# Expert tiles of a ternary mixture-of-experts layer: regrouped scale factors and a square on GpSimd

## What is computed

```python
def activation_quant(x):
    scale = 127.0 / jnp.maximum(jnp.max(jnp.abs(x), axis=-1, keepdims=True), EPS)
    return jnp.clip(jnp.round(x * scale), -128.0, 127.0) / scale

def expert_ffn(x, gw, uw, dw):
    gate = bitlinear(x, gw)
    up = bitlinear(x, uw)
    activated = up * jnp.square(jax.nn.relu(gate))
    return bitlinear(activated, dw)

logits = x @ router_w.T
probs = jax.nn.softmax(logits, axis=-1)
top_w, top_i = jax.lax.top_k(probs, TOP_K)
top_w = top_w / jnp.sum(top_w, axis=-1, keepdims=True)
combine = jnp.sum(top_w[..., None] * jax.nn.one_hot(top_i, E, dtype=x.dtype), axis=1)
for e in range(E):
    y_e = expert_ffn(x, gate_w[e], up_w[e], down_w[e])
    out = out + combine[:, e:e + 1] * y_e
```

## Time and profile before

| what | value |
|---|---|
| median of three runs | 2146.79 us (2142.44 to 2147.7) |
| the profiled execution | 2147.27 us |
| its span on the core | 2145.4 us |
| busy share PE, DVE, ACT, POOL | 81%, 75%, 55%, 28% |
| phase of the experts, scatter of the rows | 1969.5 to 2008.9 us of the span |
| loop over expert tiles, first Relu to last output | 2017.3 to 2119.4 us |

### The profile page before, as it was taken

One profiled execution on the slowest core, in us unless ns is written; L12 is line 12 of the kernel. 1 busy time (PEld: TensorE's weight loads), 2 busy tenths in 40 slices (PEclk: granted clock), 3 DMA queues, 4 the chain that ended last, 5 costly groups with the idle time before them and its releaser, 6 DMA issues.

```text
span 2145.4 us, 46365 instructions
## 1 busy us (share of the span) xinstructions
PE 1733.8 (81%) x14186; PEld 1285.6 (60%) x14186; DVE 1608.5 (75%) x4372; ACT 1181.8 (55%) x3306; POOL 601.1 (28%) x734
## 2 busy tenths in 40 slices
PE   6999999999999977756657998989889787863373
PEld 6867777777777655633335666666667566643142
DVE  4578888888888845779965888888888368874396
ACT  1156556556556524444543766666667557652393
POOL 0022222222222200001102434343443135534342
PEclk9999999999999979977777999999999879985697
DMA  2011111111111150030002222222211100000124
GB/s 104 1 34 28 29 33 28 28 33 28 28 33 28 42 121 4 1 105 1 0 8 67 56 59 59 59 59 59 64 30 36 34 11 12 12 13 14 47 78 150
DMA packets 119516, 87.66 MB, mean 41 GB/s; under 512 B 76991, under 2 KB 95746, under 8 KB 118532
## 3 DMA queue, kind: packets, MB, share of 16 engines
q1 hardware_dynamic: 116484, 80.26, 14.2%
q0 software_dynamic: 2944, 6.37, 0.9%
HBM read 72.60 MB, written 12.21 MB: 40 GB/s over the span
## 4 chain that ended last, share of the span: by engine, by line
PE 45%; DVE 25%; issue 12%; ACT 12%; POOL 2%; DMA 1%; DVEq 1%; ACTq 1%; SPq 1%; POOLq 0%
PE ps L641 4%; PE ps L663 3%; PE ps L650 3%; PE ps L679 3%; PE ps L709 3%; PE ps L612 3%; PE ps L1900 3%; PE ps L1828 2%; ACT a_pr L393 2%; PE ps L978 2%; DVE d_ks L1697 2%; PE ps L1879 2%; PE ps L1838 2%; ACT d_pr L1631 1%; POOL f_row_store L2491 1%
## 5 line engine op out<-in xcount | busy, mean ns | idle before, releaser
L393 ACT ACTIVATE a_pr<-ps,a_nm 128x257 f32<-128x257 f32 x512 | 238.2, 473 | 173.4 <-DVE a_nm L508 173.4
L516 DVE COPY a_pT<-ps 128x512 f32<-128x512 f32 x256 | 170.2, 685 | 60.0 <-PE ps L679 59.5
L1651 ACT ACTIVATE d_pr<-d_st,d_nm 128x257 f32<-128x257 f32 x256 | 128.1, 502 | 128.7 <-DVE d_nm L1760 127.4
L508 DVE TENSOR_REDUCE a_nm<-ps 128x2 f32<-128x514 f32 x256 | 174.5, 682 | 0.0
L329 POOL TENSOR_TENSOR a_sf<-a_sf,a_ratio 128x256 f32<-128x256 f32 x64 | 39.4, 616 | 472.8 <-DVE a_ratio L537 472.8
L679 PE MATMUL ps<-ident,a_pr 128*128 128x128 f32 x1024 | 159.0, 278 | 0.0
L1879 PE MATMUL ps<-d_kc,d_qc 128*128 128x257 f32 x512 | 141.8, 400 | 14.6 <-DVE d_vc L1736 14.5
L641 PE MATMUL ps<-a_cT,a_wqk 128*128 128x257 f32 x512 | 133.7, 383 | 2.9 <-DVE a_k L481 1.7
L679 PEld LDWEIGHTS ps<-ident,a_pr 128*128 128x128 f32 x1024 | 120.6, 144 | 25.7 <-issue 12.7
L1559 POOL TENSOR_TENSOR d_kc<-d_kc,d_ks 128x257 f32<-128x257 f32 x64 | 60.2, 941 | 267.8 <-ACT d_dist L1616 133.3
L650 PE MATMUL ps<-a_wvg,a_cT 128*128 128x256 f32 x512 | 129.0, 395 | 0.0
(11 more groups left out here) (385 smaller groups left out, 4491.6 us busy)
## 6 DMA issues: line engine op xcount, KB each, us to landing
a_cT<-in_ctx SPq DMA_DIRECT2D x64, 257.0 KB, 2.6
d_cT<-in_ctx SPq DMA_DIRECT2D x64, 257.0 KB, 2.8
f_wf<-in_f_w SPq DMA_DIRECT2D x24, 512.0 KB, 3.8
a_vbd<-a_vself SPq DMA_DIRECT2D x256, 8.0 KB, 1.8
d_lp<-d_pr SPq DMA_DIRECT2D x256, 0.5 KB
e_vb<-e_vs SPq DMA_DIRECT2D x256, 8.5 KB, 1.8
f_yab<-f_y_store SPq DMA_DIRECT2D x16, 256.0 KB, 5.8
c_wf<-in_c_w SPq DMA_DIRECT2D x3, 1024.0 KB, 6.9
```

Source lines behind the costliest of these rows:

```text
L393: ins = act.activation(pr[j][:, g, :], ps[:, S_BANK[u % 2] + k, S:LK], ACT.Exp, bias=nm[j][:, g:g + 1], accum_out=ssum[j][:, 0, g:g + 1])
L508: dve.tensor_reduce(nm[j][:, 2 * u:2 * u + 2], ps[:, s0:s0 + 2, S:LK], AX.X, ALU.max, negate=True).then_inc(max_ready.sem, 1)
L516: dve.tensor_copy(pT[u][:, :, :, :], ps[:, T_BANK[u % 2], :].rearrange("p (g c q) -> p g c q", g=2, c=2))\
L1651: ins = act.activation(pr[j][:, g, :], st[u][:, k, :], ACT.Exp, bias=nm[u][:, k:k + 1], accum_out=sm[j][:, g:g + 1])
```

## The change

The factors that a stored row carries are regrouped. The word at `ROW - 4` held f (the product of the squared gate scale, the up scale and the cube of the row's input scale) and now holds EPS / (127 f); the word at `ROW - 3` is multiplied by 127 f. With them the scales of a set come from three small instructions where there were five: the larger of max / 127 and the new factor, its reciprocal, and the output's scale. The routing part has four chained instructions more, and a blank row's factor is 1. The square of the odd tile moves from ACT to POOL, as a multiplication of the Relu by itself, and is put in POOL's program one set ahead of the outputs: in turn u POOL squares the odd tile of set u and then scatters the outputs of set u - 2.

```diff
-        route_link, size_link2 = chain("f_route_link", 26), chain("f_size_link2", 3)
+        route_link, size_link2 = chain("f_route_link", 30), chain("f_size_link2", 1)
...
-        rg_done, sq_done, a_done = signal("f_rg_done", 2), signal("f_sq_done", 2), signal("f_a_done", 2)
+        rg_done, a_done = signal("f_rg_done", 2), signal("f_a_done", 2)
+        sq_done = [signal(f"f_sq_done{k}") for k in range(2)]
...
-            for u in range(SETS):
-                eng.wait_ge(y_even.sem, y_even.at(u, 1))
-                eng.wait_ge(y_odd.sem, y_odd.at(u, 1))
+            for u in range(SETS + 2):
+                if u < SETS:
+                    eng.wait_ge(rg_done.sem, rg_done.at(u, 2))
+                    if u >= 1:
+                        eng.wait_ge(a_done.sem, a_done.at(u - 1, 2))
+                    eng.tensor_tensor(rg2[1][:, :], rg[1][:, :], rg[1][:, :], ALU.mult).then_inc(sq_done[1].sem, 1)
+                if u < 2:
+                    continue
+                eng.wait_ge(y_even.sem, y_even.at(u - 2, 1))
+                eng.wait_ge(y_odd.sem, y_odd.at(u - 2, 1))
                 for k in range(2):
                     eng.indirect_dma_start(y_store[:, :],
-                                           bass.IndirectOffsetOnAxis(tile_in[u % HELD][:, k, ROW - 1:ROW], 0),
+                                           bass.IndirectOffsetOnAxis(tile_in[(u - 2) % HELD][:, k, ROW - 1:ROW], 0),
...
                 act.activation(rg[k][:, :], ps[:, 2 + 2 * k, :], ACT.Relu).then_inc(rg_done.sem, 1)
-                act.wait_ge(rg_done.sem, rg_done.at(u, k + 1))
+                if k == 1:
+                    return
+                act.wait_ge(rg_done.sem, rg_done.at(u, 1))
                 if u >= 1:
-                    act.wait_ge(a_done.sem, a_done.at(u - 1, k + 1))
-                act.activation(rg2[k][:, :], rg[k][:, :], ACT.Square).then_inc(sq_done.sem, 1)
+                    act.wait_ge(a_done.sem, a_done.at(u - 1, 1))
+                act.activation(rg2[0][:, :], rg[0][:, :], ACT.Square).then_inc(sq_done[0].sem, 1)
...
-            dve.tensor_tensor(rows_f[:, :, :, ROW - 4], got[:, 2, :, :], spread(xs3[:, :], 1, 2), ALU.mult)\
+            rl.link(dve, dve.tensor_tensor(got[:, 2, :, :], got[:, 2, :, :], spread(xs3[:, :], 1, 2), ALU.mult))
+            rl.link(dve, dve.tensor_scalar(got[:, 2, :, :], got[:, 2, :, :], 127.0, None, ALU.mult))
+            rl.link(dve, dve.reciprocal(picked[:, :, :, 0], got[:, 2, :, :]))
+            dve.tensor_scalar(rows_f[:, :, :, ROW - 4], picked[:, :, :, 0], EPS, None, ALU.mult)\
                 .then_inc(scales_ready.sem, 1)
...
-            dve.tensor_tensor(rows_f[:, :, :, ROW - 3], got[:, 1, :, :], got[:, 3, :, :], ALU.mult)\
+            rl.link(dve, dve.tensor_tensor(got[:, 1, :, :], got[:, 1, :, :], got[:, 3, :, :], ALU.mult))
+            dve.tensor_tensor(rows_f[:, :, :, ROW - 3], got[:, 1, :, :], got[:, 2, :, :], ALU.mult)\
                 .then_inc(scales_ready.sem, 1)
...
-                sl.link(dve, dve.tensor_tensor(a[:, 1, :], a[:, 0, :], factors[:, :, ROW - 4], ALU.mult))
-                sl.link(dve, dve.tensor_scalar(a[:, 1, :], a[:, 1, :], EPS, None, ALU.max))
-                sl.link(dve, dve.reciprocal(a[:, 2, :], a[:, 1, :]))
+                sl.link(dve, dve.scalar_tensor_tensor(a[:, 1, :], a[:, 0, :], 1.0 / 127.0, factors[:, :, ROW - 4],
+                                                      ALU.mult, ALU.max))
                 sl.end()
-                dve.scalar_tensor_tensor(a[:, 3, :], a[:, 2, :], 127.0, factors[:, :, ROW - 4], ALU.mult, ALU.mult)\
-                    .then_inc(size_done.sem, 1)
+                dve.reciprocal(a[:, 3, :], a[:, 1, :]).then_inc(size_done.sem, 1)
                 dve.tensor_tensor(a[:, 4, :], a[:, 1, :], factors[:, :, ROW - 3], ALU.mult)
...
+    o["f_blank"][:, ROW - 4] = np.float32(1.0).view(np.int32)
```

More of the change, by code:

```diff
@@ L2546, in gate @@
                 if u >= 1:
-                    act.wait_ge(sq_done.sem, sq_done.at(u - 1, k + 1))
+                    act.wait_ge(sq_done[k].sem, sq_done[k].at(u - 1, 1))
                 act.activation(rg[k][:, :], ps[:, 2 + 2 * k, :], ACT.Relu).then_inc(rg_done.sem, 1)
-                act.wait_ge(rg_done.sem, rg_done.at(u, k + 1))
+                if k == 1:
+                    return
+                act.wait_ge(rg_done.sem, rg_done.at(u, 1))
                 if u >= 1:
-                    act.wait_ge(a_done.sem, a_done.at(u - 1, k + 1))
-                act.activation(rg2[k][:, :], rg[k][:, :], ACT.Square).then_inc(sq_done.sem, 1)
+                    act.wait_ge(a_done.sem, a_done.at(u - 1, 1))
+                act.activation(rg2[0][:, :], rg[0][:, :], ACT.Square).then_inc(sq_done[0].sem, 1)
             def turned_out(u):
@@ L2664, in products @@
                 for k in range(2):
-                    dve.wait_ge(sq_done.sem, sq_done.at(u, k + 1))
+                    dve.wait_ge(sq_done[k].sem, sq_done[k].at(u, 1))
                     if k == 0 and u >= 2:
```

## The result

The changed kernel takes 2196.03 us (median of four runs, 2190.72 to 2202.38), against 2144.61 us (median of four) for the kernel before; the ratio is 1.0244 (95% interval 1.0206 to 1.0283). It is slower, by about 52 us. The forecast was 2201 us, 2193 to 2214. The profiled execution took 2198.53 us, 51.3 us more than the one before.

A forecast was written before the change was run, and what follows sets the result against it. Two level limits, DVE's work and a loop over two sets, were taken to bound the kernel at about 4.75 us a set; 2145.4 + 1.0 - 0.7 + 53.5 = 2199.2 us of span, with 1.87 around it 2201, range 2193 to 2214.

The forecast's parts named there:

- E(u): The end of the even output that DVE makes at the very end of its turn u; POOL's transfers wait for it.
- The loop over one set: Even output, two POOL transfers, square, DVE's odd product to next even output: 7.90 us a set for 4.755, +53.5 us over 17.
- no queue effect: Rival: transfers don't hold POOL's square back and the two-set loop stays; 2147.6 us, no change, chance 0.05.
- POOL and DVE get in each other's way: Rival: POOL's square stops DVE's rounding for its whole length in each set, 17.7 us more; 2219 us, chance 0.05.
- DVE's own limit: Rival: DVE never waits, its own work limits the loop at 4.285 us a set; 2139.6 us, faster, chance 0.05.
- The first sets: Sets 0 to 2, no transfer ahead of the square: win 3 x 0.40, lose 0.46 once; -0.7 us, ends -1.2 and +1.0.
- The routing's +1.0: Added products, constant multiplication and reciprocal ahead of POOL's first scatter: +1.0 us, at most 1.3.
- The end of the span: Behind the last even output, one down product on PE at a lower clock may cost +0.7 us; taken as 0.

The follow-up runs named there:

- the unused multiplication: Regrouped scales, both squares on ACT, plus a POOL multiplication into a spare buffer nobody waits for; ratio 1.0082 to the kernel before, 5.675 us a set.
- the fill: As the run with the unused multiplication, but POOL fills 128x1024 elements with zeros and reads nothing; ratio 1.0042 to the kernel before, 5.086 us a set.
- the run with the early even output: Regrouped scales, both squares on ACT, DVE's even output straight behind the products; 2128.81 us, ratio 0.9955 to the kernel before.

## Why the prediction was right

**The queue.** The step that decided was that square(u + 1) stands behind the transfers of u - 2, and these behind E(u). The loop over one set was put at 7.90 us and is 7.83. Term by term, by the rows of the set shown above: E (2070.22) to the first transfer 0.77, as put; start to start of the transfers 1.31 for 1.29, and the second's 0.98; from transfer to square 0.01 where 0.15 was taken between 0 and 0.30; the square 1.07 for 1.04; hand-over 0.03; odd product to E 3.66 (2074.39 to 2078.05) for 3.64. 17 sets added 52.3 us for 53.5. The two runs that move one transfer and both transfers behind the square take 1.32 and 3.12 us a set away, so it is shown and not only argued.

**The rivals.** That there would be no queue effect is what the run with the outputs behind the square looks like, 4.706 us a set where 4.78 was worked out. That POOL and DVE get in each other's way was given a price of up to 1.04 a set, a chance of 0.05 and the reason that the order keeps them apart: the mechanism is real (1.16 us a set with the unused multiplication, 0.57 with the fill), and in the changed kernel it appears only in set 0. By the rule that the prediction cites for it (the Trainium skill, SBUF — State Buffer, section "Who interferes with whom"), the second to come is blocked; set 0 looks like that, but in the run with the fill the rounding that was held began 0.14 us before the fill by the record. DVE's own limit of 4.285 was put a little too high: a set took 4.262 in the run with the early even output, and there ACT has less room than DVE. No run shows where DVE's limit lies.

**The first sets were mis-sized.** They were put at -0.7 us, with ends -1.2 and +1.0, and measured +1.84, outside those ends. Here are three lines of the changed kernel, set 0's rounding, set 1's square and set 2's up products, and behind them set 2's up products in the kernel before:

```profile
2019.56 1.67 DVE L2705 TENSOR_SCALAR f_nh<-f_act,f_ams 128x512 f32<-128x512 f32 x2
...
2019.76 1.18 POOL L2499 TENSOR_TENSOR f_rg<-f_rg 128x512 f32<-128x512 f32 x1 [2.61 <-ACT f_rg L2556]
...
2022.07 3.54 PE L2790 MATMUL ps<-f_wt,f_nxT 128*128 x8 [0.17 <-issue]
```

```profile
2025.13 1.90 PE L2778 MATMUL ps<-f_wt,f_nxT 128*128 x8 [0.56 <-DVE f_act L2668]
```

The square stopped the rounding for 0.79 us, which the high end had allowed for. PE had sat idle for 2.01 us waiting for that rounding, and its next up products took 3.54 us at a granted clock of 0.53, where before they took 1.90 at 1.00; a second slow group of matmuls was not in the sum. Whether the stopped rounding brought it about stays open: in the three runs with the square on POOL and the even output in its old place, set 1's up products are slow instead (3.59 us) with no rounding stopped before them, and the same stretch is 63.8 to 64.7 us. With both squares on ACT and the even output in its old place, only set 0's are slow, as in the kernel before, and the stretch is 62.1 to 62.3 us (62.76 before).

**The small terms.** The routing's +1.0 measured +1.05; its reciprocal of twice the columns took 0.35 us, between the 0.25 of the nearest row and its double. The end of the span, taken as 0 with an end of +0.7 for a slower PE clock, grew by 0.69, about what the down product behind set 17's output took more: 1.88 us at a clock of 0.50, against 1.18.

```profile
2164.36 1.88 PE L2813 MATMUL ps<-f_wt,f_nhT 128*128 x8 [6.14 <-DVE f_ys L2713]
```

The prediction took 1.21 us for the eight matmuls before; that is the busy time of eleven, and its 0.7 isn't changed by it. The 4.5 us by which the layers ahead were faster in this execution are no part of the change; without them the sum of 2199.2 us would have stood beside 2201.2. It is luck that the misses of +2.5 in the first sets and -1.2 in the 17 sets partly cancel.

## What to carry to other kernels

Before work goes to an engine that is mostly idle, read what the idle time is: an engine that waits in its program for the end of a turn is no free engine, and what stands behind that wait is late by all that stands ahead of it. Put work that others wait for ahead of the long waits and the transfers in the queue, and check that the loop through the engine's queue order is shorter than the present turn. GpSimd beside a busy VectorE also stops some of VectorE's instructions, so a square that takes 0.64 us off ACT can put 0.79 us on a rounding of DVE where they meet.

## Not expected

- In most sets of the run with the unused multiplication, DVE's small step began some 0.6 us before POOL's multiplication is recorded to begin, while POOL was in a transfer, and still ended with the multiplication. In the run with the fill, the same step passed beside the transfer in 0.16 us. Why a multiplication that is queued behind a transfer stops the step so early stays open; a record of POOL's start that is late would explain it too.
- From the end of an indirect transfer to a multiplication on POOL it is 0.01 us, but 0.30 to the next transfer.
